# First attention of a two-layer decoder as a pipeline over single tiles, and the router's group ranks by halving

## Chip, cores and metric

The program runs on 1 core of one Trainium2 chip, in one launch. The metric is device time in microseconds (us) of that core, median of three runs for the kernel before.

## The reference, cut to what matters

The decoder has 8192 tokens (128 sequences of 64) of 128 features. It runs seven parts one after the other; two of them are touched here. The first attention replaces softmax by positive features of queries and keys (16 heads of 64):

```
q, k, v = x@Wq, x@Wk, x@Wv                      # 16 heads x 64
dash    = (data * 64**-0.25) @ proj.T
diag    = sum(data**2) * 64**-0.5 / 2
qf      = exp(dash - diag - max(dash, per head)) + 1e-6
kf      = exp(dash - diag - max(dash, over all)) + 1e-6
kv      = einsum('bnhm,bnhd->bhmd', kf, v)      # sums over the 64 tokens
num     = einsum('bnhm,bhmd->bnhd', qf, kv)
den     = einsum('bnhm,bhm->bnh', qf, sum(kf))
y1      = x + (num / den) @ Wo                  # then layer norm and feed forward
```

The last layer's router scores 64 experts for each token, in 8 groups of 8. A group's rank is the sum of its two best scores; the four best groups are kept, and the eight best experts in them.

```
group_scores = top_k(sfc.reshape(T, 8, 8), 2)[0].sum(-1)
_, gidx      = top_k(group_scores, 4)
```

## The kernel before

The tokens are 64 tiles of 128 (two sequences each). Every stage is a `Phase` with a program for each engine, written out by hand; engines meet at semaphores, and between two stages all engines meet at a barrier. So the order of the work on an engine is the order of the code.

`phase_performer` is the first attention. It handles two tiles (U = 2) per pass of its loop, 32 passes. Each projection of a tile (`wide`) is six matmuls of 512 columns: two halves of the 1024 features, three products each of high and low f16 parts. The five projections are q (Wq), k (Wk), v (Wv), and, through weights joined with `proj` beforehand, the features before the exponent (Wqp and Wkp). Each result fills two of the eight banks of PSUM. A pair of tiles has the buffers a0, b0, a1, b1, which are all eight banks, and every product of a tile goes through its own a or b: q and the query features first, then k over the query features, the transposed query features over q, and so on down to the output. The trace prints them as `b_a` and `b_b` without number. Since all banks belong to the pair in hand, TensorE starts q of a tile of the next pass only behind this line, when the tile's predecessor in the same buffers has been read for the last time:

```
pe.wait_ge(y_ready, before(it, j))
```

For each tile VectorE sums the squares of q (L567), takes the maximum per head (L569), joins both (L572), subtracts them from the query features (L574), sums the squares of k (L578), scales them (L580), subtracts them from the key features (L583), adds 1e-6 (L587), copies half of the sums over keys (L424), takes the reciprocals of den (L594, twice), multiplies (L597, twice) and adds x (L606). ScalarE squares q (L533), takes the exponent of the query features (L536), squares k (L540), copies the transposed query features (L543), takes the exponent of the key features (L546), copies v (L548), copies the other half of the sums (L551) and the transposed values (L555). TensorE's small products are: transposes of the query features (L479), sums over keys (L497), sums over features (L509), transposes of the values (L515), output (L520). The code runs each step for both tiles, then the next step for both.

The router's part is `rank_groups` in `phase_cross1`, the stage of the second layer's cross attention. A batch k is four tiles (N = 4), 16 batches in all; its steps on VectorE are spread over four columns of that stage's own pipeline, between the attention's steps. `after(k, step)` is a wait on VectorE's own semaphore plus an increment. The ranks of a batch take one MAX8 for every tile and group (32 of 8 elements each, eight sorted values out), then an addition of the first two.

## Time and profile before

| | us |
|---|---|
| runs of the kernel before | 4549.0 median, 4544.06 to 4552.46 (3 runs) |
| the profiled execution: its own time | 4554.91 |
| its span, first to last instruction | 4552.8 |
| first attention, 130 to 1158 us of the span | 1028.00 |
| TensorE busy in it | 835.96 |
| VectorE busy in it | 608.06 |
| ScalarE busy in it | 491.20 |
| stage with the router, 2880 to 3460 us | 580.00 |

The span lies 2.1 us below the time of its own execution, and that execution 5.9 us above the median. Busy time counts an instruction from its start to its modelled end; neighbours overlap, so the time from one start to the next says more of what an engine needs.

### The profile page before, as it was taken

What the parts mean: (1) busy time and instruction counts of PE and PEld (TensorE: products, weight loads), DVE (VectorE), ACT (ScalarE), POOL (GpSimd) and SP (SyncE); (2) the same over time, 40 slices, a digit from 0 to 9 for tenths busy, and PEclk for the clock granted to TensorE, in tenths of its full rate; (3) what the DMA queues carried; (4) which work ended last, traced back from release to release, by engine and by line L of the source; (5) the groups of instructions that cost most, each with busy time, mean ns of one, the idle gap of its engine ahead of it and who ended that gap; (6) DMA issues with size and microseconds to landing.
All of it is one profiled execution on the core that took longest, in us unless ns stands there. A gap on an engine that the chain in (4) does not pass through costs nothing. (4 is left out here: it accounts for less than half of the span.)

```text
span 4552.8 us, 96381 instructions
## 1 busy us (share of the span) xinstructions
PE 3746.1 (82%) x30771; PEld 2413.5 (53%) x30771; DVE 3298.2 (72%) x7642; ACT 2475.4 (54%) x6025; POOL 1914.2 (42%) x2753
## 2 busy tenths in 40 slices
PE   7788888888676777649898999788875999999998
PEld 3455555555444555436666666577762444444443
DVE  6655556565565666448888888588886888888888
ACT  1344444444664555337777777555544555555555
POOL 1000000000454666436556556111114778778777
PEclk9999999999886555556767777888877999999999
DMA  2000000000111111020000000122217566556664
GB/s 72 7 9 7 9 9 7 9 7 9 46 49 42 37 37 37 26 41 15 16 14 14 14 14 10 46 53 54 53 41 166 136 136 143 133 133 140 136 137 92
DMA packets 288788, 245.48 MB, mean 54 GB/s; under 512 B 60920, under 2 KB 216604, under 8 KB 288540
## 3 DMA queue, kind: packets, MB, share of 16 engines
q1 hardware_dynamic: 279452, 239.85, 22.2%
q10 hardware_dynamic: 9216, 4.20, 0.3%
q8 instruction: 55, 0.90, 0.1%
q14 instruction: 65, 0.53, 0.0%
HBM read 210.40 MB, written 33.55 MB: 54 GB/s over the span
## 5 line engine op out<-in xcount | busy, mean ns | idle before, releaser
L2536 POOL TENSOR_TENSOR d_hidden<-d_gated,d_upper 128x512 f32<-128x512 f32 x528 | 801.5, 1543 | 233.9 <-DVE d_upper L2645 110.3
L2652 DVE TENSOR_TENSOR d_h_low<-d_hidden,d_h_high 128x512 f16<-128x512 f32 x528 | 542.1, 1027 | 118.5 <-ACT d_h_high L2612 117.3
L2606 ACT ACTIVATE d_gated<-d_g 128x512 f32<-128x512 f32 x528 | 315.3, 597 | 466.1 <-PE d_u L2552 466.1
L684 POOL MEMSET f_minus_half<- 128x4 f32 x1 | 0.1, 102 | 1029.3 <-POOLq L37 1029.3
L2645 DVE TENSOR_TENSOR d_upper<-d_u,d_coef 128x512 f32<-128x512 f32 x512 | 349.4, 683 | 32.5 <-DMA d_coef<-coefT 13.0
L2612 ACT ACTIVATE d_h_high<-d_hidden 128x512 f16<-128x512 f32 x528 | 328.4, 622 | 8.2 <-POOL d_hidden L2536 8.2
L1719 ACT ACTIVATE c_sc<-c_sc,c_negmax 128x129 f32<-128x129 f32 x1024 | 326.1, 393 | 12.1 <-issue 9.5
L1547 POOL TENSOR_TENSOR c_posg<-w_pos,c_gate 128x512 f32<-128x512 f32 x256 | 265.7, 1038 | 0.0
L2550 PE MATMUL d_g<-d_x_high,w_Wg_high 128*128 128x512 f16 x528 | 200.9, 381 | 75.4 <-DVE d_upper L2645 38.4
L1626 PE MATMUL c_turned<-all_ident,c_sc 128*128 128x128 f32 x1024 | 232.4, 368 | 5.3 <-ACT c_sc L1719 4.8
L1724 ACT ACTIVATE c_pT<-c_turned 128x512 f32<-128x512 f32 x256 | 149.6, 584 | 154.7 <-PE c_turned L1626 154.7
L2550 PE MATMUL d_o<-d_h_high,w_Wd_high 128*128 128x512 f16 x528 | 200.1, 379 | 1.6 <-ACT d_h_high L2612 1.6
L2551 PE MATMUL d_u<-d_x_high,w_Wu_low 128*128 128x512 f16 x528 | 200.9, 380 | 0.0
L2550 PE MATMUL d_u<-d_x_high,w_Wu_high 128*128 128x512 f16 x528 | 200.8, 380 | 0.0
L2552 PE MATMUL d_g<-d_x_low,w_Wg_high 128*128 128x512 f16 x528 | 200.8, 380 | 0.0
L2551 PE MATMUL d_g<-d_x_high,w_Wg_low 128*128 128x512 f16 x528 | 200.8, 380 | 0.0
L2552 PE MATMUL d_u<-d_x_low,w_Wu_high 128*128 128x512 f16 x528 | 200.7, 380 | 0.0
L2552 PE MATMUL d_o<-d_h_low,w_Wd_high 128*128 128x512 f16 x528 | 200.1, 379 | 0.0
L2551 PE MATMUL d_o<-d_h_high,w_Wd_low 128*128 128x512 f16 x528 | 200.1, 379 | 0.0
L2048 POOL TENSOR_SCALAR d_rstd<-d_mv 128x1 f32<-128x1 f32 x64 | 13.9, 217 | 434.6 <-DVE d_mv L2269 434.6
L533 ACT ACTIVATE b_sq<-b_a 128x1024 f32<-128x1024 f32 x64 | 65.5, 1023 | 229.8 <-PE b_a L160 229.8
L1626 PEld LDWEIGHTS c_turned<-all_ident,c_sc 128*128 128x128 f32 x1024 | 150.8, 184 | 62.0 <-issue 50.2
(396 smaller groups left out, 10918.7 us busy)
## 6 DMA issues: line engine op xcount, KB each, us to landing
d_coef<-coefT SPq DMA_DIRECT2D x256, 512.0 KB, 7.7
d_cT<-in_ctxT SPq DMA_DIRECT2D x128, 64.0 KB, 2.0
mx_x<-in_xT SPq DMA_DIRECT2D x16, 256.0 KB, 2.8
b_x<-in_x SPq DMA_DIRECT2D x64, 64.0 KB, 1.8
y<-b_y SPq DMA_DIRECT2D x64, 64.0 KB, 1.6
f_y<-y SPq DMA_DIRECT2D x16, 256.0 KB, 3.3
f_x<-in_x SPq DMA_DIRECT2D x16, 256.0 KB, 3.9
x<-f_res SPq DMA_DIRECT2D x16, 256.0 KB, 2.4
```

The lines of the kernel that those rows point to most:

```text
L1547: nc.gpsimd.tensor_tensor(posg[a][:], w["pos"][:, hs, :], gate[s][:, hs].unsqueeze(2).to_broadcast([T, 4, T]), ALU.mult).then_inc(posg_rea ...
L1626: last = nc.tensor.transpose(tbank[a % 2][:, i, :], sc[slot(j)][:, 4 * a + i, 0:T], w["ident"][:])
L1719: last = nc.scalar.activation(sc[s][:, h, :], sc[s][:, h, :], ACT.Exp, bias=negmax[s][:, h:h + 1], scale=SCALE)
L1724: nc.scalar.activation(pT[slot(j)][:, 4 * a:4 * a + 4, :], tbank[a % 2][:], ACT.Copy).then_inc(pT_copied, 1)
L2536: nc.gpsimd.tensor_tensor(hidden[b][:], gated[b][:], upper[b][:], ALU.mult).then_inc(h_ready, 1)
L2550: nc.tensor.matmul(out, weights[0], high, start=start, stop=False)
L2551: nc.tensor.matmul(out, weights[1], high, start=False, stop=False)
L2552: return nc.tensor.matmul(out, weights[0], low, start=False, stop=stop)
L2606: nc.scalar.activation(gated[b][:], ps_g[i][:], ACT.Silu, scale=1.0 / W_SCALE).then_inc(silu_ready, 1)
L2612: nc.scalar.activation(h_high[b][:], hidden[b][:], ACT.Copy).then_inc(h_high_ready, 1)
L2645: nc.vector.tensor_tensor(upper[b][:], ps_u[i][:], coef[c % CBUFS][:, u % CU, :], ALU.mult).then_inc(upper_ready, 1)
L2652: nc.vector.tensor_tensor(h_low[b][:], hidden[b][:], h_high[b][:], ALU.subtract).then_inc(h_low_ready, 1)
```

## The change

`phase_performer` becomes a pipeline over single tiles. Column c of the pipeline does the projections and features of tile c, the sums over keys and over features of tile c-1 (`behind1`) and the normalising, transposing, output and addition of x of tile c-2 (`behind2`). The banks are dealt by role: `ps_a` takes q, then v, then k, then the transposed query features; `ps_b` takes the query features, then the key features; `ps_c` and `ps_d` take both kinds of sums, and `ps_d` the transposed values and the output. In SBUF every tensor keeps two slots. The products, their shapes and their number stay the same; TensorE, ScalarE, VectorE and the DMA queue get a new order, and the waits follow from it. There are 66 columns: four written out, a loop of 29 passes over two columns, four written out. Stores of y run two columns behind the loads of x, in the queue order store, load.

In the router, the 32 MAX8 and the addition of a batch become eleven operations over all groups at once: halves of a group are compared (4 with 4, 2 with 2, 1 with 1) and `high` and `low` carry the best and second best found so far. `after` has five steps where it had two before the ranks are added, and all later steps are renumbered.

```diff
--- before.py
+++ after.py
-        ps_a = [ph.ps(f"a{j}", [P, 2, 512]) for j in range(U)]
-        ps_b = [ph.ps(f"b{j}", [P, 2, 512]) for j in range(U)]
...
+        ps_a, ps_b, ps_c, ps_d = (ph.ps(n, [P, 2, 512]) for n in ("a", "b", "c", "d"))
...
+        def pipelined(eng, step):
+            def column(it, j):
+                step(*(None if isinstance(it, int) and not 0 <= U * it + j - back < TILES else (it, j - back) for back in range(3)))
+            for j in range(2 * U):
+                column(0, j)
+            with eng.Fori(2, steps - 1) as it:
+                for j in range(U):
+                    column(it, j)
+            for j in range(U + 2):
+                column(steps - 1, j)
...
+                def store(it, j):
+                    s, tile = slot(j), tile_of(it, j)
+                    sp.wait_ge(y_ready, nth(it, j))
+                    sp.sem_inc(waited, 1)
+                    sp.dma_start(y1[tile, :], y[s][:]).then_inc(stored[s], 16)
+                def load(it, j):
+                    sp.dma_start(x_sb[slot(j)][:], x[tile_of(it, j), :]).then_inc(loaded[slot(j)], 16)
+                def step(column, behind1, behind2):
+                    run(store, behind2)
+                    run(load, column)
+                pipelined(nc.sync, step)
...
+                def project_q(it, j):
+                    if not is_early(it, j, 1):
+                        pe.wait_ge(qfT_copied, nth(it, j) - 1)
+                    wide(it, j, ps_a, Wq).then_inc(q_ready, 1)
+                def features_q(it, j):
+                    if not is_early(it, j, 1):
+                        pe.wait_ge(dk_shifted, nth(it, j) - 1)
+                    wide(it, j, ps_b, Wqp).then_inc(dq_ready, 1)
+                def project_k(it, j):
+                    pe.wait_ge(v_copied, nth(it, j))
+                    wide(it, j, ps_a, Wk).then_inc(k_ready, 1)
+                def features_k(it, j):
+                    pe.wait_ge(dq_shifted, nth(it, j))
+                    wide(it, j, ps_b, Wkp).then_inc(dk_ready, 1)
+                def project_v(it, j):
+                    pe.wait_ge(q_squared, nth(it, j))
+                    wide(it, j, ps_a, Wv).then_inc(v_ready, 1)
+                def turn_features(it, j):
+                    pe.wait_ge(k_squared, nth(it, j))
+                    pe.wait_ge(q_exp, nth(it, j))
...
+                    last.then_inc(qfT_ready, 1)
+                def sum_keys(it, j):
+                    s = slot(j)
+                    pe.wait_ge(kf_ready, nth(it, j))
+                    if not is_early(it, j, 1):
+                        pe.wait_ge(y_ready, nth(it, j) - 1)
+                    pe.sem_inc(waited, 1)
...
+                    last.then_inc(kv_ready, 1)
+                def sum_features(it, j):
+                    s = slot(j)
+                    pe.wait_ge(kv0_copied, nth(it, j))
+                    pe.wait_ge(kv1_copied, nth(it, j))
+                    pe.sem_inc(waited, 1)
...
+                    last.then_inc(num_ready, 1)
+                def turn_values(it, j):
+                    pe.wait_ge(attn_done, nth(it, j))
...
+                    last.then_inc(turned, 1)
+                def output(it, j):
+                    pe.wait_ge(attn_ready, nth(it, j))
...
+                    last.then_inc(proj_ready, 1)
+                def step(column, behind1, behind2):
+                    run(features_q, column)
+                    run(project_q, column)
+                    run(turn_values, behind2)
+                    run(project_v, column)
+                    run(output, behind2)
+                    run(project_k, column)
+                    run(sum_keys, behind1)
+                    run(features_k, column)
+                    run(turn_features, column)
+                    run(sum_features, behind1)
+                pipelined(nc.tensor, step)
...
+                def step(column, behind1, behind2):
+                    run(square_q, column)
+                    run(copy_values, behind2)
+                    run(copy_v, column)
+                    run(exp_q, column)
+                    run(square_k, column)
+                    run(copy_sums, behind1)
+                    run(copy_features, column)
+                    run(exp_k, column)
+                pipelined(nc.scalar, step)
...
+                def norm_k(it, j):
+                    s = slot(j)
+                    dve.wait_ge(k_squared, nth(it, j))
+                    nc.vector.tensor_reduce(kn[s][:], sq[s][:], AX, ALU.add).then_inc(kn_ready, 1)
+                    dve.wait_ge(kn_ready, nth(it, j))
...
+                def shift_q(it, j):
+                    s = slot(j)
+                    dve.wait_ge(qn_ready, nth(it, j))
+                    dve.wait_ge(topped, nth(it, j))
+                    dve.sem_inc(waited, 1)
+                    nc.vector.scalar_tensor_tensor(q_shift[s][:], qn[s][:], DIAG, top[s][:], ALU.mult, ALU.add).then_inc(q_shift_ready, 1)
+                    dve.wait_ge(q_shift_ready, nth(it, j))
+                    nc.vector.tensor_tensor(e_sb[s][:], heads(ps_b), q_shift[s][:].unsqueeze(2).to_broadcast([P, H, DH]), ALU.subtract).then_inc(dq_shifted, 1)
...
+                def step(column, behind1, behind2):
+                    run(normalise, behind2)
+                    run(max_q, column)
+                    run(add_eps, behind1)
+                    run(norm_q, column)
+                    run(shift_q, column)
+                    run(add_x, behind2)
+                    run(copy_sums, behind1)
+                    run(norm_k, column)
+                    run(shift_k, column)
+                pipelined(nc.vector, step)
...
-                ROUTER_STEPS = 14
+                ROUTER_STEPS = 18
...
                 def rank_groups(k):
                     after(k, 1)
-                    for n in range(N):
-                        for g in range(G):
-                            last = nc.vector.max(best2[:, n, g, :], biased[:, n, 8 * g:8 * g + 8])
-                    last.then_inc(router_own, 1)
-                    after(k, 2)
-                    nc.vector.tensor_tensor(groups[:, :, 0:G], best2[:, :, :, 0], best2[:, :, :, 1], ALU.add).then_inc(router_own, 1)
-                    after(k, 3)
+                    eights = biased[:].rearrange("p n (g e) -> p n g e", g=G)
+                    nc.vector.tensor_tensor(high[0][:], eights[:, :, :, 0:4], eights[:, :, :, 4:8], ALU.max)
+                    nc.vector.tensor_tensor(low[0][:], eights[:, :, :, 0:4], eights[:, :, :, 4:8], ALU.min).then_inc(router_own, 1)
+                    for i in range(1, 3):
+                        a, b = slice(0, 4 >> i), slice(4 >> i, 8 >> i)
+                        after(k, 2 * i)
+                        nc.vector.tensor_tensor(mid[i][:], high[i - 1][:, :, :, a], high[i - 1][:, :, :, b], ALU.min)
+                        nc.vector.tensor_tensor(low[i][:], low[i - 1][:, :, :, a], low[i - 1][:, :, :, b], ALU.max).then_inc(router_own, 1)
+                        nc.vector.tensor_tensor(high[i][:], high[i - 1][:, :, :, a], high[i - 1][:, :, :, b], ALU.max)
+                        after(k, 2 * i + 1)
+                        nc.vector.tensor_tensor(low[i][:], low[i][:], mid[i][:], ALU.max).then_inc(router_own, 1)
+                    after(k, 6)
+                    nc.vector.tensor_tensor(groups[:, :, 0:G], high[2][:, :, :, 0], low[2][:, :, :, 0], ALU.add).then_inc(router_own, 1)
+                    after(k, 7)
...
```

TensorE in the loop of `phase_performer`, before, at the seam of two passes: transposes of the values of both tiles into a, output of both into b, and then q of the next pass into a. Of every `wide` the rows are L158, L159, L160, twice.

```order
L515 MATMUL b_a<-all_ident,b_attn 128x128 x16
L520 MATMUL b_b<-w_Wo,b_attnT 128x128 x16
L58 UNCONDITIONAL_BRANCH
L58 ISA
L158 ISA
L158 MATMUL b_a<-w_Wq_high,parts_xT_high 128x512
L159 MATMUL b_a<-w_Wq_low,parts_xT_high 128x512
L160 REGISTER_ALU
L160 MATMUL b_a<-w_Wq_high,parts_xT_low 128x512
```

TensorE in the loop after, around the output of tile c-2: it stands between v and k of tile c.

```order
L158 MATMUL b_a<-w_Wv_high,parts_xT_high 128x512
L159 MATMUL b_a<-w_Wv_low,parts_xT_high 128x512
L160 MATMUL b_a<-w_Wv_high,parts_xT_low 128x512
L537 MATMUL b_d<-w_Wo,b_attnT 128x128 x8
L158 MATMUL b_a<-w_Wk_high,parts_xT_high 128x512
L159 MATMUL b_a<-w_Wk_low,parts_xT_high 128x512
L160 MATMUL b_a<-w_Wk_high,parts_xT_low 128x512
```

Moved are the output (L520, now L537), out of a run of both tiles' small products into the middle of another tile's projections, and k and v, which now share the buffer a with q.

VectorE in the loop before: the k half of both tiles, from the sums of squares of k to the copies of sums (REGISTER_ALU rows make the value a wait compares with).

```order
L578 TENSOR_REDUCE b_stat<-b_sq 128x16
L85 REGISTER_ALU
L580 TENSOR_SCALAR b_stat<-b_stat,w_key_max 128x16
L85 REGISTER_ALU
L583 TENSOR_TENSOR b_kf<-b_a,b_stat 128x1024
L578 TENSOR_REDUCE b_stat<-b_sq 128x16
L85 REGISTER_ALU
L580 TENSOR_SCALAR b_stat<-b_stat,w_key_max 128x16
L85 REGISTER_ALU
L583 TENSOR_TENSOR b_kf<-b_a,b_stat 128x1024
L587 TENSOR_SCALAR b_kf<-b_kf 128x1024 x2
L424 COPY b_kv<-b_a 128x520 x2
```

VectorE in the loop after: the whole of a column but the reciprocals and products of tile c-2, which stand ahead of these rows; L609 and L643 belong to tile c-1, L663 to tile c-2.

```order
L624 TENSOR_REDUCE b_top<-b_b 128x16
L609 TENSOR_SCALAR b_kf<-b_kf 128x1024
L613 TENSOR_REDUCE b_qn<-b_sq 128x16
L631 SCALAR_TENSOR_TENSOR b_q_shift<-b_qn,b_top 128x16
L633 TENSOR_TENSOR b_e<-b_b,b_q_shift 128x1024
L660 REGISTER_ALU
L662 ISA
L663 TENSOR_TENSOR b_y<-b_d,b_x 128x128
L643 COPY b_kv<-b_c 128x520
L618 TENSOR_REDUCE b_kn<-b_sq 128x16
L620 TENSOR_SCALAR b_k_shift<-b_kn,w_key_max 128x16
L639 TENSOR_TENSOR b_kf<-b_b,b_k_shift 128x1024
```

Moved are the additions of 1e-6 (L587, now L609) and of x (L606, now L663) in between the query steps of tile c, and the copy of sums (L424, now L643) ahead of the sums of squares of k.

VectorE in `phase_cross1` before, at the ranks of a batch:

```order
L2252 TENSOR_TENSOR d_attn<-d_back,d_den 128x128
L2288 MAX d_best<-d_biased 128x8 x32
L2291 TENSOR_TENSOR d_groups<-d_best 128x4x8
L2294 MAX d_gtop<-d_groups 128x8 x4
L2257 TENSOR_TENSOR d_kB<-d_kT,w_variant 128x512
```

and after, in the same place:

```order
L2356 TENSOR_TENSOR d_high<-d_biased 128x128
L2357 TENSOR_TENSOR d_low<-d_biased 128x128
L2361 TENSOR_TENSOR d_mid<-d_high 128x64
L2362 TENSOR_TENSOR d_low<-d_low 128x64
L2363 TENSOR_TENSOR d_high<-d_high 128x64
L2365 TENSOR_TENSOR d_low<-d_low,d_mid 128x64
L2361 TENSOR_TENSOR d_mid<-d_high 128x32
L2362 TENSOR_TENSOR d_low<-d_low 128x32
L2363 TENSOR_TENSOR d_high<-d_high 128x32
L2365 TENSOR_TENSOR d_low<-d_low,d_mid 128x32
L2367 TENSOR_TENSOR d_groups<-d_high,d_low 128x4x8
L2370 MAX d_gtop<-d_groups 128x8 x4
```

The 32 MAX8 have given way to ten comparisons of 128, 64 and 32 elements, and the addition reads their results; what stands behind is the same.

## Rows read from the trace of the kernel before

**Rows 1.** The page's head and the granted clock, 40 equal slices of the span.

```profile
span 4552.8 us, 96381 instructions
...
PEclk9999999999886555556767777888877999999999
```

**Rows 2.** Busy time by stage; columns as its first line says, PEclk granted.

```profile
core 0: us, PE busy (x) PEld busy (x) DVE busy (x) ACT busy (x) POOL busy (x), PEclk, DMA share, GB/s
...
130.00:1158.00 1028.00, 835.96 (x12160) 555.46 (x12160) 608.06 (x896) 491.20 (x512) 0.82 (x2) 0.98 0.03 8
...
2880.00:3460.00 580.00, 434.24 (x4608) 380.65 (x4608) 450.12 (x1729) 307.49 (x923) 68.43 (x200) 0.78 0.22 60
```

**Rows 3.** Waits from 130 to 1158 us: total, times, longest.

```profile
ACT b_sq L533 <- PE b_a L160: 229.8, 64, 59.3
DVE b_y L606 <- PE b_b L520: 143.0, 64, 3.2
```

**Rows 4.** Timeline of VectorE, 480 to 545 us: start, length, instruction, idle before.

```profile
486.59 0.29 DVE L606 TENSOR_TENSOR b_y<-b_b,b_x 128x128 f32<-128x128 f32 x1 [3.16 <-PE b_b L520]
...
493.21 1.22 DVE L574 TENSOR_TENSOR b_e<-b_b,b_stat 128x1024 f32<-128x1024 f32 x1
...
500.20 1.22 DVE L578 TENSOR_REDUCE b_stat<-b_sq 128x16 f32<-128x1024 f32 x1 [2.04 <-ACT b_sq L540]
501.45 0.23 DVE L580 TENSOR_SCALAR b_stat<-b_stat,w_key_max 128x16 f32<-128x16 f32 x1
503.73 1.23 DVE L583 TENSOR_TENSOR b_kf<-b_a,b_stat 128x1024 f32<-128x1024 f32 x1 [2.04 <-PE b_a L160]
504.87 1.21 DVE L578 TENSOR_REDUCE b_stat<-b_sq 128x16 f32<-128x1024 f32 x1
...
510.94 0.70 DVE L424 COPY b_kv<-b_a 128x520 f32<-128x520 f32 x1 [0.66 <-PE b_b L497]
...
518.15 0.29 DVE L606 TENSOR_TENSOR b_y<-b_b,b_x 128x128 f32<-128x128 f32 x1 [3.16 <-PE b_b L520]
```

**Rows 5.** Timeline of ScalarE, 480 to 545 us.

```profile
489.56 1.02 ACT L533 ACTIVATE b_sq<-b_a 128x1024 f32<-128x1024 f32 x1 [3.92 <-PE b_a L160]
```

**Rows 6.** Timeline of TensorE, 482 to 512 us in pieces: first matmuls of runs.

```profile
483.49 0.98 PE L515 MATMUL b_a<-all_ident,b_attn 128*128 128x128 f32 x7 [0.42 <-DVE b_attn L597]
...
484.42 0.72 PE L520 MATMUL b_b<-w_Wo,b_attnT 128*128 128x128 f32 x5
...
487.99 0.38 PE L158 MATMUL b_a<-w_Wq_high,parts_xT_high 128*128 128x512 f16 x1
...
494.50 0.39 PE L158 MATMUL b_b<-w_Wk_high,parts_xT_high 128*128 128x512 f16 x1 [1.16 <-DVE b_e L574]
...
504.74 0.38 PE L158 MATMUL b_b<-w_Wv_high,parts_xT_high 128*128 128x512 f16 x1
...
506.03 0.38 PE L158 MATMUL b_b<-w_Wv_high,parts_xT_high 128*128 128x512 f16 x1
...
509.72 0.24 PE L497 MATMUL b_a<-b_v,b_kf 64*64 64x65 f32 x1 [0.20 <-ACT b_v L548]
...
510.67 0.22 PE L509 MATMUL b_a<-b_kv,b_qfT 64*64 64x65 f32 x1
```

**Rows 7.** Granted clock in stretches of 4 us, columns as in rows 2.

```profile
544.00:548.00 4.00, 3.00 (x56) 2.63 (x48) 2.51 (x6) 1.30 (x2) 0.00 (x0) 1.00 0.00 0
972.00:976.00 4.00, 1.74 (x8) 0.66 (x7) 2.96 (x4) 1.33 (x2) 0.00 (x0) 0.96 0.00 0
976.00:980.00 4.00, 3.98 (x20) 3.02 (x17) 1.45 (x2) 3.01 (x4) 0.00 (x0) 0.62 0.00 0
```

**Rows 8.** Timeline of VectorE around one ranking of groups in the router.

```profile
3013.61 2.27 DVE L2288 MAX8 d_best<-d_biased 128x8 f32<-128x8 f32 x32
3016.03 0.22 DVE L2291 TENSOR_TENSOR d_groups<-d_best 128x32 f32<-128x32 f32 x1
...
3024.16 0.29 DVE L2264 TENSOR_TENSOR d_y<-d_back,d_x_again 128x128 f32<-128x128 f32 x1
```

305 lines of the change are left out of this document (118 added, 187 removed).

## Prediction

> **What bounds the kernel now.** I read first the page's head, for the span and the clock [rows 1], then the busy times by stage [rows 2], since the change touches two stages alone. The first attention takes 1028 us, 23% of the span. No engine fills it: TensorE is busy 836 us, VectorE 608, ScalarE 491. So engines wait for each other, and the waits say how [rows 3]: ScalarE stands 230 us before it may square q, and VectorE 143 us before the last addition, both for TensorE. The timelines show the same place once per pass. The additions of x that end two passes lie 31.56 us apart (486.59 and 518.15 in [rows 4]), 15.78 us a tile. After the output TensorE starts q of the next pass at 487.99 [rows 6] and ScalarE can do nothing before 489.56 [rows 5]: when a pass ends and the next begins, one engine works and two stand.
>
> What TensorE needs for a tile follows from starts, not from busy time [rows 6]. A projection of six matmuls: 504.74 to 506.03, 1.29 us, five of them 6.45. Eight transposes: 483.49 to 484.42, 0.93, twice 1.86. Output of two tiles: 484.42 to 487.99, 1.785 each. Sums over keys: 509.72 to 510.67, 0.95; sums over features are as many matmuls of the same shape, 0.95. Together 12.0 us of 15.78. That is the floor: no product goes away. VectorE's instructions come to 608/64 = 9.5 us a tile, ScalarE's to 7.7 [rows 2]; neither can become the bound by its work.
>
> 32 passes of 31.56 us are 1010, so 18 of the 1028 us are something else: the start at a low clock, the edges, and falls of the clock. I counted twelve stretches of 4 us or pairs of them with a granted clock well below 1.00; one is 976 to 980 at 0.62, behind a stretch in which TensorE was busy 1.74 of 4 us [rows 7].
>
> **The change, part by part.** The new period is the longest closed chain through the three orders. I start a column with the query features at 0 on TensorE and take each time from a row.
> - q starts at 1.29, ScalarE squares it 1.57 later (487.99 to 489.56, [rows 5, 6]), at 2.86, for 1.02, to 3.88.
> - A handover to TensorE costs 0.07 (493.21 + 1.22 = 494.43 on VectorE, 494.50 on TensorE, [rows 4, 6]). v waits for the squares, as both use `ps_a`: 3.95. The transposes of tile c-2 (0.93) lie in that gap, from 2.58 to 3.51, so TensorE idles 0.44.
> - Then without a wait: output at 5.24, k at 7.02, sums over keys at 8.31.
> - VectorE copies them 1.22 after their start (509.72 to 510.94): 9.53. The sums of squares of k follow 0.09 before the copy's end, as 504.87 lies before 503.73 + 1.23 [rows 4]: 9.53 + 0.70 - 0.09 = 10.14. k was squared by 7.02 + 1.57 + 1.02 = 9.61, in time.
> - Scaling them starts 1.25 later (500.20 to 501.45), 11.39; the subtraction 0.23 + 0.03 later, 11.65; it lasts 1.23, to 12.88.
> - The next column's query features need `ps_b` back: 12.88 + 0.07 = 12.95.
>
> **So 12.95 us a tile**, 0.95 over the floor, in two idle pieces of 0.44 and about 0.5. The added waits hold the following. Query features of c wait for the key features of c-1 (this chain). Sums over keys wait for the addition of x of c-2, with the key features queued behind: output ends near 7.1, the addition 0.29 later, and the sums are due only at 8.31. Output waits for ScalarE's copy of the values: 2.58 + 1.1 + 1.02 = 4.7, and it is due at 5.24. q waits for the copy of the transposed features; these start at 10.55, so that is done near 12.7, before 14.24. In SP's queue each load stands behind a store that waits for y; it is wanted two columns later, 26 us. These are hidden; the thinnest cover is 0.5 us, and a copy 0.6 late would add 0.1 a tile, 6 us in all.
>
> 64 x 12.95 = 829. The last tile's rest beyond its column: in the old pass 8.7 us lie between its sums over keys and the end of an addition (509.72 to 518.44), with the exponent and 1e-6 ahead; I take 12, between 5 (TensorE's part alone) and 31 (a whole old pass). Of the 18 us of other time I keep 6: the start and the edges stay, but the falls followed idle stretches that the new column does not have; in 4 us of it TensorE stands at most 0.9. Stage: 829 + 12 + 6 = **847, 181 less**.
>
> **The router.** 32 MAX8 take 2.27 us, 0.07 apart, and with the gap of a wait the addition starts at 2.42 (3013.61 to 3016.03, [rows 8]). A `tensor_tensor` of 128 elements lasts about 0.29 and one of 32 about 0.22 [rows 8]; 64, not shown, lies between, 0.25. Independent ones overlap by 0.08, and `after` costs 0.15 of gap (3015.88 to 3016.03). Two of 128: 0.50; gap 0.15; the three of 64 and the dependent one 0.78, the wait between them mostly under the third; gap 0.15; the same of 32, 0.70; gap 0.15. Sum 2.43 against 2.42. If no overlap happened and all five gaps showed, the addition would come at 3.2, 0.8 us later; if more overlapped, 0.1 earlier. In 16 batches: 0, between -2 and +13 us. I take 0: the overlaps are visible in this stage.
>
> The sum against the profiled execution: 4554.9 - 181 = 4373.9 us. The median of the runs is 5.9 lower, so **4368**.
>
> **The rivals.**
> - *Longer handovers.* The chain has four places where one engine waits for another and two where VectorE waits for itself. Some waits are double now (sums over keys, subtraction). If each of the seven steps cost 0.13 more, the period is 13.85, 58 us more, 4426. If a further chain closes behind the loop, such as the copy of values late, 15 us is thinkable: 4499. For it speaks that a column mixes engines that the old pass kept in long runs; against it that the handovers of [rows 4 to 6] already stand beside other engines' work.
> - *The floor.* If the two idle pieces vanish, 64 x 12.0 = 768, stage 786, 4307. The chain above forbids it unless steps are shorter than their rows.
> - *The clock falls: slower.* TensorE becomes the bound, so its clock decides: the period is 12.0/c. At c = 0.76 it is 15.8 and the gain is gone; below that the kernel is slower than before. The slices of other stages go down to 0.5 to 0.7 [rows 1], and the router's stage has 0.78 with TensorE busy 434 of 580 us [rows 2]. If small pauses made it swing half of the time between 1.2 and 2.4 GHz, c = 0.75: 16.0 a tile, stage 1042, 4563; at 0.6 it is 4817. Against it: 544 to 548 us has TensorE busy 3.00 of 4 us, with small f32 products, at 1.00, and the falls came behind longer idleness [rows 7].
> - *It doesn't overlap.* If columns ran one tile after another as now, nothing changes: 4549. The waits of the code don't ask for that.
>
> The Trainium skill, page "TensorE: Matmul & The Clock Gate", section "A second HAM failure mode: psum-queue depth-cycling", speaks for the third: a kernel that cycles through PSUM banks leaves TensorE short idle times between groups of matmuls, and its clock then swings between the two levels. The new column has two such idle times. By the page the result would be the 4563 of that rival. The trace disagrees so far: handovers through the same banks in the old pass left the clock at 1.00 in the row named.
>
> **How the numbers follow.** Forecast 4335 to 4410: 0.74. Longer handovers, 4410 to 4520: 0.16. Clock, slower: 0.05. No overlap: 0.02. Below 4335, towards the floor: 0.03. A range of 4335 to 4435 holds the first and about half of the second, 0.82. 0.2%, 9 us, is about what a measurement of this kernel tells from no change. Faster: 0.74 + 0.16 + 0.03 = 0.93; same 0.02; slower 0.05.
>
> **What would show it.** In the changed trace, additions of x 12.95 us apart, one per tile; v starting 0.07 behind the squares of q, with 0.4 us idle ahead; query features starting behind the subtraction of the key features; granted clock 1.00 all through the stage; stage near 847 us; the ranks' addition 2.4 us after their first comparison. I would be wrong if TensorE's longest wait stood elsewhere (output, sums over keys), or if matmuls of 512 columns started 0.43 instead of 0.215 us apart for more than the stage's start.

## The result, and the profile after

The changed kernel takes 4405.1 us (median of 4 runs, 4399.8 to 4407.7) against 4550.7 us for the kernel before on the same chip: ratio 0.9675, 95% interval 0.9663 to 0.9687. The forecast was 4368, its range 4335 to 4435: inside the range and 37 us above the number. Of these 37 us, 26 are in the profiled executions, and they are the matter of what follows. The other 11 come from the step between profile and median: the profiled execution of the kernel before lay 5.9 us above its median, that of the changed kernel (4399.8) lies 5.3 below.

The page's head and the granted clock of the changed kernel, as in [rows 1]:

```profile
span 4397.7 us, 96050 instructions
...
PEclk9999999997865555577777777988869999999999
```

Busy time of the changed kernel in stretches, columns as in [rows 2]. The first row is the whole stage of the first attention:

```profile
130.00:996.00 866.00, 816.49 (x12160) 546.10 (x12160) 610.28 (x896) 500.93 (x512) 1.91 (x3) 0.99 0.04 10
...
200.00:300.00 100.00, 95.89 (x1398) 64.18 (x1400) 71.76 (x105) 59.05 (x61) 0.00 (x0) 1.00 0.03 10
...
700.00:800.00 100.00, 95.66 (x1374) 64.04 (x1375) 72.80 (x109) 59.46 (x62) 0.00 (x0) 1.00 0.03 9
```

The stage fell from 1028 us to 866, with the same instructions on every engine, and TensorE is busy 94% of it. The clock is 1.00 in each of the six stretches of 100 us from 200 to 800, of which two stand here.

The additions of x, which tell the period: the changed kernel's row in the list by tile, first over the whole stage and then from 560 to 700 us (shortest/median/longest ns, first and last start).

```profile
L663 DVE TENSOR_TENSOR b_y<-b_d,b_x x64: 290/292/293, 166.6 to 995.7; 128x128 f32<-128x128 f32 x64
...
L663 DVE TENSOR_TENSOR b_y<-b_d,b_x x11: 290/292/292, 562.5 to 694.4; 128x128 f32<-128x128 f32 x11
```

One addition per tile: (995.7 - 166.6)/63 = 13.16 us over the stage, (694.4 - 562.5)/10 = 13.19 in the middle of it. In [rows 4] a tile took 15.78; the forecast was 12.95. These are means. Single additions lie 12.96 and 13.42 apart by turns (509.72, 522.68 and 536.10 below), since a pass of the loop holds two columns; the 12.96 alone is not the forecast come true.

The changed kernel's timeline of TensorE, the first matmul of each run in one column and of the next column, as in [rows 6]:

```profile
502.28 0.39 PE L158 MATMUL b_b<-w_Wqp_high,parts_xT_high 128*128 128x512 f16 x1 [0.27 <-DVE b_kf L639]
...
503.58 0.38 PE L158 MATMUL b_a<-w_Wq_high,parts_xT_high 128*128 128x512 f16 x1
...
506.24 0.39 PE L158 MATMUL b_a<-w_Wv_high,parts_xT_high 128*128 128x512 f16 x1 [0.32 <-ACT b_sq L561]
...
507.54 1.95 PE L537 MATMUL b_d<-w_Wo,b_attnT 128*128 128x128 f32 x16
509.33 0.38 PE L158 MATMUL b_a<-w_Wk_high,parts_xT_high 128*128 128x512 f16 x1
...
510.72 0.27 PE L514 MATMUL b_c<-b_v,b_kf 64*64 64x65 f32 x1
...
515.51 0.39 PE L158 MATMUL b_b<-w_Wqp_high,parts_xT_high 128*128 128x512 f16 x1 [0.27 <-DVE b_kf L639]
```

ScalarE squaring q in this column and in the next:

```profile
505.16 1.03 ACT L561 ACTIVATE b_sq<-b_a 128x1024 f32<-128x1024 f32 x1 [1.92 <-PE b_a L160]
...
518.31 1.03 ACT L561 ACTIVATE b_sq<-b_a 128x1024 f32<-128x1024 f32 x1 [1.85 <-PE b_a L160]
```

VectorE in the same column, from the addition of x through the subtraction that frees `ps_b`, and the two additions behind it:

```profile
509.72 0.29 DVE L663 TENSOR_TENSOR b_y<-b_d,b_x 128x128 f32<-128x128 f32 x1 [0.66 <-PE b_d L537]
511.95 0.70 DVE L643 COPY b_kv<-b_c 128x520 f32<-128x520 f32 x1 [1.94 <-PE b_d L514]
512.56 1.21 DVE L618 TENSOR_REDUCE b_kn<-b_sq 128x16 f32<-128x1024 f32 x1
513.81 0.23 DVE L620 TENSOR_SCALAR b_k_shift<-b_kn,w_key_max 128x16 f32<-128x16 f32 x1
514.15 1.23 DVE L639 TENSOR_TENSOR b_kf<-b_b,b_k_shift 128x1024 f32<-128x1024 f32 x1
...
522.68 0.29 DVE L663 TENSOR_TENSOR b_y<-b_d,b_x 128x128 f32<-128x128 f32 x1 [0.47 <-PE b_d L537]
...
536.10 0.29 DVE L663 TENSOR_TENSOR b_y<-b_d,b_x 128x128 f32<-128x128 f32 x1 [0.66 <-PE b_d L537]
```

Read these together from 502.28: it is the forecast's chain, link by link. q 1.30 later; ScalarE squares it from 505.16 to 506.19 and v starts at 506.24, 3.96 (forecast 3.95); output at 5.26 (5.24); k 7.05 (7.02). Then the links grow. Sums over keys at 8.44 (8.31), so 1.39 us behind k where a projection takes 1.29. The copy 1.23 and the reduction 0.61 behind are as forecast. The subtraction comes 0.34 behind the scaling, forecast 0.26. It ends at 515.38, and the query features start 0.13 later, forecast 0.07. Three links give 0.10 + 0.08 + 0.06 = 0.24 us a column. The column shown is 13.23 us long (502.28 to 515.51), with 0.04 more in small steps; the next is 13.15, as ScalarE starts 1.49 behind q there (516.82 to 518.31) and not 1.58 (forecast 1.57). The two alternate, and their mean is the 13.19.

Waits of the changed kernel from 130 to 996 us, which answer to [rows 3]:

```profile
ACT b_sq L561 <- PE b_a L160: 181.1, 64, 62.9
DVE b_kv L643 <- PE b_d L514: 130.0, 64, 2.4
...
DVE b_y L663 <- PE b_d L537: 46.2, 64, 6.1
...
PEld b_a L158 <- ACT b_sq L561: 35.6, 64, 2.1
...
PE b_b L158 <- DVE b_kf L639: 17.9, 63, 1.8
```

TensorE's two named waits (PEld is its weight loads) are those of the forecast: for the squares of q ahead of v, and for the subtraction ahead of the query features.

The router, the changed kernel's VectorE around one ranking, as in [rows 8]:

```profile
2853.24 0.29 DVE L2356 TENSOR_TENSOR d_high<-d_biased 128x128 f32<-128x128 f32 x1
...
2853.88 0.23 DVE L2361 TENSOR_TENSOR d_mid<-d_high 128x64 f32<-128x64 f32 x1
2854.02 0.22 DVE L2362 TENSOR_TENSOR d_low<-d_low 128x64 f32<-128x64 f32 x1
...
2855.54 0.19 DVE L2367 TENSOR_TENSOR d_groups<-d_high,d_low 128x32 f32<-128x32 f32 x1
```

The addition starts 2.30 us behind the first comparison, in all 16 batches between 2.28 and 2.31; before it was 2.42 (2.40 to 2.42).

**What the forecast had no term for** stands in the last stage, the experts, whose code the change does not touch. First the weight load of `d_g`, by tile, of the kernel before and of the changed one, then of the changed kernel ScalarE's waits from 3330 to 4330 us and the instruction queue in the whole stage (3276 to 4398 us):

```profile
L2550 PEld LDWEIGHTS d_g<-d_x_high,w_Wg_high x528: 95/98/151, 3461.1 to 4535.7; 128*128 128x128 f16 x176
```

```profile
L2626 PEld LDWEIGHTS d_g<-d_x_high,w_Wg_high x528: 95/98/152, 3296.3 to 4380.6; 128*128 128x128 f16 x176
```

```profile
ACT d_gated L2682 <- PE d_u L2628: 406.8, 467, 2.3
ACT d_gated L2682 <- issue: 22.6, 5, 6.4
```

```profile
q14 instruction: 44, 0.36, 0.1%
```

From the first to the last load 1084.3 us, before 1074.6: 10 us more for the same work. ScalarE stood five times, 4.5 us each on average, with nothing to wait for that the profile shows, some 137 us apart. The loop's branch is met six times, from 3562.1 to 4248.3 us; the stands follow the five that lead back to its start and not the last. Queue 14, which carries instructions in packets of 8 KB, moved 44 of them, against 18 in the kernel before (3440 to 4553 us; 20 with the two at the program's end), which has no such stand of ScalarE. Between 3660 and 4360 us, in the middle of the loop, the kernel before has 3 of its packets, the changed one 5 or 6 in every 140 us.

### The profile page after: what moved, and what is told of

Same layout as the page of the kernel before. It is cut to its first block and busy times, and to the rows that moved or that the text cites. A ratio compares the mean times of both kernels' runs of the same rounds, so it can differ in the third digit from the quotient of the medians.

```text
span 4397.7 us, 96050 instructions
## 1 busy us (share of the span) xinstructions
PE 3699.9 (84%) x30771; PEld 2374.2 (54%) x30771; DVE 3292.1 (75%) x7290; ACT 2486.9 (57%) x6025; POOL 1921.4 (44%) x2753
## 5 line engine op out<-in xcount | busy, mean ns | idle before, releaser
L1692 PE MATMUL c_turned<-all_ident,c_sc 128*128 128x128 f32 x1024 | 214.9, 346 | 16.8 <-ACT c_sc L1785 14.8
L1897 DVE TENSOR_REDUCE c_top<-c_sc 128x4 f32<-128x516 f32 x256 | 176.9, 691 | 8.8
L1692 PEld LDWEIGHTS c_turned<-all_ident,c_sc 128*128 128x128 f32 x1024 | 139.8, 173 | 76.9 <-issue 41.9
```

The source lines that it names most:

```text
L1692: last = nc.tensor.transpose(tbank[a % 2][:, i, :], sc[slot(j)][:, 4 * a + i, 0:T], w["ident"][:])
L1897: m = own.mark(nc.vector.tensor_reduce(top[s][:, hs], sc[s][:, hs, :], AX, ALU.max))
```

## The experiments

All ran beside the kernel before, and a ratio is to its runs on the same chip, whose medians were 4549.0 to 4553.2 us. A single run has no interval. "Last stage" is from the first to the last weight load of `d_g`; the expectations count from the end of the stage before to the end of the program, 37 us more. "Packets" are those of queue 14 from the first such load to the end. The period is that of the additions of x in the middle of the stage.

| kernel | median us (runs) | ratio to before, 95% | period | last stage | packets |
|---|---|---|---|---|---|
| before | 4550.7 (4) | | 15.78 | 1074.6 | 20 |
| changed | 4405.1 (4) | 0.9663 to 0.9687 | 13.19 | 1084.3 | 44 |
| attn_only | 4407.1 (5) | 0.9672 to 0.9697 | | 1092.8 | 44 |
| router_only | 4571.4 (6) | 1.0032 to 1.0056 | | 1101.6 | 44 |
| router_pad86 | 4553.6 (11) | 0.9994 to 1.0014 | | 1071.6 | 20 |
| pad88 | 4383.2 (5) | 0.9621 to 0.9646 | | 1075.9 | 19 |
| q_first | 4372.1 (5) | 0.9599 to 0.9624 | 12.76 | 1090.0 | 44 |
| q_first_pad88 | 4355.6 (5) | 0.9555 to 0.9581 | | 1073.0 | 19 |
| norm_k_twice | 4482.9 (1) | | 14.38 | 1089.0 | 44 |
| norm_q_twice | 4410.1 (1) | | 13.26 | 1092.0 | 44 |
| wait_moved | 4398.2 (1) | | 13.20 | 1084.7 | 44 |
| turn_first | 4374.3 (5) | 0.9595 to 0.9621 | 12.95 | 1073.3 | 19 |
| pad24 | 4407.3 (1) | | | 1092.5 | 44 |
| pad256 | 4413.4 (1) | | | 1090.2 | 44 |

### One part at a time

attn_only is the new first attention with the old ranks; router_only the old attention with the new ranks. The edit is the change's own pieces, for attn_only:

```diff
-                    nc.vector.tensor_tensor(high[0][:], eights[:, :, :, 0:4], eights[:, :, :, 4:8], ALU.max)
...
+                    for n in range(N):
+                        for g in range(G):
+                            last = nc.vector.max(best2[:, n, g, :], biased[:, n, 8 * g:8 * g + 8])
```

> The new attention with the router's old ranks. Theory: the gain is the attention's alone; columns 13.2 us apart as in the full change, the stage 161 us shorter than before, and the last stage (experts), whose code nobody touched, some 10 us longer than before, since ScalarE's program is the same 40 instructions longer as in the full change. Total about 145 us below before. Rival (the ranks carry part of it): the stage with the router was 7 us shorter after the change, so without the new ranks this kernel would lie 7 us above the full change. By the ranks' own timeline (0.15 us a batch) only 2 us.

> The old attention with the new ranks. By the ranks' own timeline, 0.15 us for each of 16 batches: 2 us less than before, within noise. By the stage's length in the two traces: 7 us less. Last stage as before, since ScalarE's program has the length of before: no reloads of instructions in its loop.

The attention alone gives 4407.1, the whole change 4405.1: it is the gain. Its last stage is 18 us longer than before in the profiled execution, where some 10 were expected. The ranks alone, expected 2 to 7 us faster, make the kernel slower, 4571.4, by 0.3 to 0.6%, although the addition comes 2.30 us behind the first comparison there too. Their loss is not in the router's stage but in the last one, 1101.6 against 1074.6 us. VectorE's waits there in router_only, then in the run below that mends it (3480 to 4500 us):

```profile
DVE d_upper L2655 <- issue: 27.4, 5, 5.7
DVE d_upper L2655 <- PE d_u L2562: 10.5, 20, 1.5
```

```profile
DVE d_upper L2657 <- PE d_u L2564: 5.4, 15, 0.5
```

Here it is VectorE that stands five times. Its program has 86 instructions fewer than before, ScalarE's is unchanged.

### Where the last stage's loop stands

The theory: what the change alters for the last stage is only where its code lies. ScalarE's loop of 341 instructions starts at its instruction 1833 in the kernel before and at 1873 in the changed one; VectorE's, 312 long, starts at 2804 before, 2781 in the changed kernel and 2718 in router_only. The padding is increments of a semaphore that nobody waits for:

```diff
                 pipelined(nc.scalar, step)
+                for _ in range(88):
+                    act.sem_inc(waited, 1)
```

In router_pad86 the same stands at the end of VectorE's first attention, with 86 and `dve.sem_inc`; in pad24 and pad256 the number is 24 and 256.

> The full change with 88 increments of a semaphore on ScalarE behind its last step of the attention; nothing else. Everything behind stands 88 instructions later in ScalarE's program, 128 later than before in all. Theory: the last stage got longer because ScalarE's loop there (341 instructions) now straddles one more piece of its instruction memory and is loaded again in every pass (43 packets on queue 14 in that stage against 17); shifted to a multiple of 128 it should not be: about 17 packets, stage 10 us shorter, total 8 us below the full change (88 increments cost 2 to 4 us at the seam). Rival (chance, or the memory traffic of that execution): no change of the packets, and the time equal or 3 us longer.

> The kernel before with the new ranks of the router alone, and 86 semaphore increments at the end of VectorE's first-attention program, so that VectorE's loop of the last stage stands at the same instruction (2804) as in the kernel before; nothing of the work is left out. Theory of placement (the new ranks make VectorE's program 86 instructions shorter, the loop of the last stage then starts at 2718 and its instructions are fetched again in every pass): the five waits for an instruction stream ahead of the upper part in that stage, 27 us together, go away, the last stage takes 1112 us instead of 1139, about 20 instruction packets on queue 14 in it instead of 44, and the median falls from 4571 to 4546 to 4552, ratio to before near 1.000. Rival (the last stage is longer by the new ranks' data or by chance of the execution): it stays at 4571, ratio 1.0044. The 86 increments themselves cost at most 86 times 0.06 us, 5 us, once.

> The whole change with 24 semaphore increments at the end of ScalarE's first-attention program, so that its loop of the last stage starts at instruction 1897; nothing of the work is left out. One look: the last stage and its packets on queue 14 count. Starts at 1833 and 1961 gave about 1112 us and 20 packets, a start at 1873 gave 1121 to 1130 us and 44. If the loop of 341 instructions is fetched again in every pass when it lies over three blocks of 256 instructions and not when it lies over two, then 1833, 1873 and 1961 put the border so that 1897 is bad as well: 44 packets, five instruction waits on ScalarE, last stage 1121 to 1130. If any pause or any padding cures it, 20 packets and 1112.

> The whole change with 256 semaphore increments in the same place, so that the loop starts at 2129, which is 1873 plus 256; nothing of the work is left out. One look, the last stage counts (the increments themselves may cost up to 20 us once, at the end of the first attention). If blocks of 256 instructions decide, the place is as bad as that of the whole change: 44 packets and 1121 to 1130 us, although 88 increments gave 19 packets and 1113. If a longer distance from the start of the program is what helps, or any padding, 20 packets and 1112.

88 increments take 22 us off the changed kernel (19 if each is compared through its own kernel before), where 8 were expected, and the packets above those of before go too. 86 on VectorE bring router_only back to the time of before: 4553.6 against 4553.2 on that chip, just over the 4546 to 4552 expected. 24 leave ScalarE's loop at 1897 with 44 packets and five stands of 3.7 to 5.9 us (the profile puts one down to TensorE), and 256, which put it at 2129 = 1873 + 256, are as bad as none. So neither a pause nor the amount of padding cures it: the place does. ScalarE's waits in the last stage of pad24, then of pad256:

```profile
ACT d_gated L2684 <- issue: 20.2, 4, 5.9
```

```profile
ACT d_gated L2684 <- issue: 23.8, 5, 5.7
```

Starts at 1833 and 1961 are good, 1873, 1897 and 2129 bad. The Trainium skill, page "Runtime: NRT & Kernel Launch", section "Instruction fetch mechanics", says that most engines hold two blocks of 256 instructions and that a branch to a block outside them has to fetch it first. By that rule a loop of 341 fits when it lies over two blocks and not when it touches a third, and all five starts fit one position of the borders (bad when the start plus 91 to 130, modulo 256, is over 171); the trace agrees, in the eight profiled kernels with a bad start of ScalarE's loop alone as in router_only. What the profiles show without the rule: a bad place of ScalarE's loop makes the last stage 8 to 21 us longer in one execution, and costs 22 us by the medians of the changed kernel and pad88.

The paddings have a price of their own, read from the stages behind: from the last addition of x to the first `b_bn` two stages on, the feed-forward stage between, it takes 12 us more in pad256 and 8 more in router_pad86, and in pad88 nothing. The traces record the increments themselves: on ScalarE they start 0.07 us apart (256 from 988.97 to 1006.78 us), on VectorE 0.10 (86 from 1156.29 to 1164.60). ScalarE is done with its tiles before VectorE and TensorE, and the 6 us that the 88 of pad88 take cost nothing.

### Is the chain closed?

Two kernels give VectorE the same extra work, 1.21 us a column, at two places. norm_k_twice:

```diff
+                    nc.vector.tensor_reduce(spare[s][:], sq[s][:], AX, ALU.add)
                     nc.vector.tensor_reduce(kn[s][:], sq[s][:], AX, ALU.add).then_inc(kn_ready, 1)
```

norm_q_twice has the same ahead of the reduction into `qn`.

> The whole change, with the sums of squares of k taken twice per column (the first into a tile that nobody reads); the result is the same. One look: the period of the columns in the first attention counts. If the closed chain is right, in which these sums stand between the copy of the sums over keys and the scaling with nothing to hide them, the period grows from 13.2 us by the whole of the second reduction: by its 1.25 us of time from start to start, less nothing, to 14.4, and the stage from 866 to about 943. Rival (TensorE's own work is the bound and the chain has slack): the period grows by less than 0.4.

> The whole change, with the sums of squares of q taken twice per column (the first into a tile that nobody reads); the result is the same. One look. VectorE gets as much more work as when the sums of k are taken twice, but ahead of the shift of the query features, where TensorE's key features wait next at 9.3 us of the column. By the chain the period stays at 13.2 to 13.4 us if the shift of the query features and the addition of x have that much slack. If VectorE's total work were the bound the period would grow by about 1.2, as with k.

Additions of x by tile, 560 to 700 us, first of norm_k_twice, then of norm_q_twice:

```profile
L665 DVE TENSOR_TENSOR b_y<-b_d,b_x x9: 290/292/293, 573.6 to 688.6; 128x128 f32<-128x128 f32 x9
```

```profile
L665 DVE TENSOR_TENSOR b_y<-b_d,b_x x11: 280/281/283, 565.4 to 698.0; 128x128 f32<-128x128 f32 x11
```

(688.6 - 573.6)/8 = 14.38 against (698.0 - 565.4)/10 = 13.26: on k the period grows by 1.19, on q by 0.07, out of the same work. Between its first and its second sums norm_k_twice shows what each column pays:

```profile
576.44 1.21 DVE L619 TENSOR_REDUCE b_spare<-b_sq 128x16 f32<-128x1024 f32 x1
577.57 1.21 DVE L620 TENSOR_REDUCE b_kn<-b_sq 128x16 f32<-128x1024 f32 x1
```

The start-to-start of 1.13 is nearly all of the 1.19. The chain over the sums of k is closed with no slack, and VectorE's total work is not the bound.

### Breaking the chain

q_first lets TensorE issue q ahead of the query features, so that the subtraction has 1.29 us more before anything waits for it:

```diff
                 def step(column, behind1, behind2):
-                    run(features_q, column)
                     run(project_q, column)
+                    run(features_q, column)
```

> The full change with TensorE's column begun by q and then the query features. Theory (closed chain): what holds the column is the chain from the query features over q, v, output, k, sums over keys, the copy, sums of squares of k and the subtraction back to the query features; q does not need the buffer that this chain frees, so q first takes 1.3 us out of the way and the column falls from 13.2 to about 12.75 us, 27 us in all, held then by TensorE's own work and the wait for the squares of q. Rival (TensorE is full already, the idle time is only how its starts are drawn): 13.2 us and no gain.

> The whole change, with q issued before the query features on TensorE, and with 88 semaphore increments at the end of ScalarE's first-attention program; nothing of the work is left out. If the two gains found apart (33 us by the order in the column, 22 by ScalarE's placement) have separate causes they add up: 4405 - 33 - 22 = 4350, last stage 1113 us, attention stage 834. If the gain of the padding came from something else in the run, it does not add: 4372.

The additions of x of q_first, 560 to 700 us, and TensorE's waits from 200 to 800, of its weight loads and of its matmuls:

```profile
L663 DVE TENSOR_TENSOR b_y<-b_d,b_x x11: 278/278/280, 570.9 to 698.5; 128x128 f32<-128x128 f32 x11
```

```profile
PEld b_d L537 <- ACT b_attnT L590: 14.7, 47, 0.3
...
PE b_a L158 <- ACT b_qfT L578: 9.4, 47, 0.2
```

The period is 12.76, and the wait for the subtraction is gone. Two others show now: output's for the copy of the values, which the forecast had covered by 0.5 us, 0.31 a time, and q's for the copy of the transposed query features, 0.20 a time. Which of the two would have to go first was not tried. The stage takes 834 us (130 to 964), 32 less, where 27 were expected: 0.43 x 64 is 27.5, the rest lies at its edges. With the padding the two gains add up nearly: 4355.6 against the 4350 expected, ratio 0.9568, the fastest version here.

### The small links

wait_moved tries to take back the 0.08 ahead of the subtraction, which has two waits:

```diff
                     dve.wait_ge(kn_ready, nth(it, j))
...
+                    dve.wait_ge(dk_ready, nth(it, j))
...
                 def shift_k(it, j):
-                    dve.wait_ge(dk_ready, nth(it, j))
                     dve.wait_ge(k_shift_ready, nth(it, j))
```

(The added line stands ahead of the wait for `kn_ready` in `norm_k`.)

> The whole change, with VectorE's wait for the key features moved up from ahead of the subtraction to ahead of the scaling of the sums of squares, where it stands behind a 1.21 us reduction; nothing of the work is left out. One look, the period of the columns counts. If the subtraction starts 0.34 us behind the scaling, and not 0.26 as in the kernel before, because two waits stand ahead of it, the gap goes back to 0.26 and, as the chain has no slack, the period falls from 13.2 by the same 0.08 to 13.1, the stage by 5 us. Rival (the 0.34 is the size of the operands or the pool's semaphore, not the second wait): 0.34 and 13.2 stay.

VectorE in wait_moved:

```profile
576.94 1.21 DVE L618 TENSOR_REDUCE b_kn<-b_sq 128x16 f32<-128x1024 f32 x1
578.26 0.23 DVE L621 TENSOR_SCALAR b_k_shift<-b_kn,w_key_max 128x16 f32<-128x16 f32 x1
578.52 1.23 DVE L639 TENSOR_TENSOR b_kf<-b_b,b_k_shift 128x1024 f32<-128x1024 f32 x1
```

The subtraction now follows the scaling by 0.26, as hoped, but the scaling follows the reduction by 1.32 instead of 1.25, and the period stays at 13.20. The half of the expectation on the gap held, the half on the period failed: a reduction of 1.21 us ahead does not hide the wait.

Nor is the number of waits the cause. The kernel before waits twice ahead of its subtraction too, for the key features and for its own scaling. Where both were there in time the subtraction came 0.27 behind the scaling:

```profile
506.12 0.23 DVE L580 TENSOR_SCALAR b_stat<-b_stat,w_key_max 128x16 f32<-128x16 f32 x1
506.39 1.23 DVE L583 TENSOR_TENSOR b_kf<-b_a,b_stat 128x1024 f32<-128x1024 f32 x1
```

Of two waits one stands in an instruction of its own, which the timeline leaves out and the trace records. In the kernel before it is the wait for TensorE's key features, passed at 506.13 while the scaling ran. In the changed kernel it is the wait for VectorE's own scaling: it starts at 514.08, 0.27 behind the scaling, and the subtraction follows 0.07 later. In wait_moved a wait of this kind, for VectorE's own reduction, stands ahead of the scaling (578.19, the scaling at 578.26). So the 0.07 belongs to a wait for the engine's own last result that stands by itself, and moving the other wait within the chain moved it along. A version with that wait on the subtraction itself was not run.

turn_first adds to q_first_pad88 the moved wait, and turns the query features ahead of the key features:

```diff
                     run(sum_keys, behind1)
-                    run(features_k, column)
                     run(turn_features, column)
+                    run(features_k, column)
```

> q ahead of the query features, ScalarE's 88 semaphore increments and the moved wait as in the runs of their names, and on TensorE the turning of the query features ahead of the key features, so that these cover less and the transposes fall into the time in which VectorE works at the sums of k; nothing of the work is left out. With q first the period is 12.76 us. By starts read from its trace the closed chain then runs over ScalarE's squares, VectorE's shift of the query features and their exponent; with the transposes moved up I expect 12.65 us, 7 us off the stage, and the moved wait hidden: 4348, between 4340 and 4356. If the transposes wait for the exponent of the query features (0.3 us late or more), the period grows and the run is slower than 4356.

The expectation of 4340 to 4356 failed. It took 4374.3 us, 19 more than q_first_pad88 on another chip (ratio 0.9608 against 0.9568), period (699.1 - 569.6)/10 = 12.95; 64 times the difference in the period is 12 us. TensorE in turn_first:

```profile
571.78 1.09 PE L502 MATMUL b_a<-all_ident,b_e 128*128 128x128 f32 x8 [0.24 <-ACT b_sq L566]
572.71 0.38 PE L158 MATMUL b_b<-w_Wkp_high,parts_xT_high 128*128 128x512 f16 x1
```

The transposes do wait, not for the exponent as the expectation's second case had it but for the squares of k, with which they share `ps_a`, and the key features queue behind them. The exponent has its part all the same: ScalarE starts these squares at 570.72, at the end of the exponent (569.76, 1.06 long), without a wait between. VectorE then waits 0.78 for these ahead of the scaling: the moved wait has made it stand earlier too. How much of the loss is due to either edit wasn't tried apart.

## Why the prediction was right, and where it was short

**The mechanism held step by step.** Column by column, one addition per tile; v starts 0.05 behind the squares of q, query features behind the subtraction, the chain's order as forecast, and norm_k_twice against norm_q_twice shows that this chain and not VectorE's work sets the period. The 4374 us of profiled time that the sum gave compare with 4399.8 of the profiled execution, 26 more: 19 in the first attention, 10 in the last stage, 8 less in the router's, and 5 more spread over the stretches between. That the last stage and the router's nearly cancel is luck: the forecast had 0 for either.

**The period, 12.95 forecast, 13.19 measured: 0.24 x 64 = 15 us.** The step that was short is the pricing of three links by rows of the old pass: the small sums of 64 rows started 1.39 us behind the first matmul of k, not 1.29; the subtraction 0.34 behind the scaling, not 0.23 + 0.03; the query features 0.13 behind its end, not 0.07. The prediction took each of these steps from a place where what lengthens it here was absent. The second is the wait for VectorE's own scaling that stands by itself, as the records of the changed kernel and of wait_moved show (above). The third looks alike: the wait for the subtraction stands in a register instruction of its own (515.41, 0.05 long) and the first weight load at 515.51 behind it, while ahead of v, as at 494.50 in the kernel before, the weight load itself waits. For the first the wait was over 0.67 us earlier (the sums over keys wait for the addition of x, done at 510.01); what comes late is the weight load of 64 rows, 0.52 behind the last one of k:

```profile
510.19 0.10 PEld L160 LDWEIGHTS b_a<-w_Wk_high,parts_xT_low 128*128 x1
510.71 0.13 PEld L514 LDWEIGHTS b_c<-b_v,b_kf 64*64 64x64 f32 x1 [0.42 <-issue]
```

A load of 128 rows follows the last one of the key features by 0.22 in the same column (512.69 to 512.90). No run puts the first or the third to the test. The prediction had named a direction ("some waits are double now") and put it in a rival at 0.13 for each of seven steps. It was three steps at 0.06 to 0.10, and the reason given was wrong: both steps named there, sums over keys and subtraction, wait twice in the kernel before as well.

**Edges and falls of the clock, 12 + 6 us forecast:** 865.7 - 64 x 13.19 = 21.5 for both. Stage 847 against 866: 15 from the period, 4 from here.

**The clock rival did not come.** 1.00 in all of 200 to 800 us, where TensorE is busy 96 of each 100 us and stands twice a column, 0.32 and 0.27 in the rows above. By the Trainium skill, page "TensorE: Matmul & The Clock Gate", section "A second HAM failure mode: psum-queue depth-cycling", weighed in the prediction, the 4563 us of that rival would have come; the trace disagrees, since the new column cycles through the same banks with short idle pieces at a granted clock of 1.00. The floor of 4307 did not come either, and its 12.0 us a tile was too low: it has 0.95 for each kind of small sums, where the sums over keys alone add 1.39 - 1.29 + 1.09 = 1.19. Adding the shortest steps of the changed kernel, q_first and turn_first gives 12.4 (an estimate for a column without any wait), and q_first, with two waits left, came to 12.76.

**The router, 0 forecast:** the addition comes 0.12 us sooner, 2 us in 16 batches, as the sum of 2.43 for the new ranks was 0.13 too high. The stage shows somewhat more: from ScalarE's first to its last `d_res` 490.0 us against 497.5, and in the other profiles 487.2 to 493.0 with the new ranks and 494.5 in attn_only with the old. By medians they are worth 2 us beside the new attention (4405.1 against 4407.1, which is within what the runs scatter) and some 8, the price of the padding, in router_pad86. So 2 to 8 us, at or below the low end of the -2 to +13 given; what beyond the 2 at the addition makes them stays open.

**The last stage, no term in the forecast:** 10 us in the profiled execution, 22 by the medians of pad88 and the changed kernel. The prediction costed what the changed parts do and never what they do to code behind them. Both parts move the experts' loops: the attention moves ScalarE's to a bad place, the ranks alone move VectorE's to one, and together VectorE's is at a good one, which is why attn_only and the whole change are alike and router_only is slow. With the placement mended the change takes 4383.2 us, against 4368 forecast. The 15 us that remain are as many as the period's; the smaller terms (4 at the edges, 5 between the stages, 8 less in the router's) about cancel.

## What to carry to other kernels

When a change makes a program longer or shorter, look at the loops behind it: compare the instruction packets in their stretch and the waits put down to "issue", before a difference of some tenths of a per cent is read as the worth of the edit. An edit that gained a little in its own stage was +0.4% here for this reason alone, and 88 idle increments were worth 0.4 to 0.5%.

In a pipeline over engines, write the longest closed chain and count each wait in it at its price, those that stand in an instruction of their own above all; then test it by the same extra work once on the chain and once beside it. What to change next is the order at the place where the chain closes (q_first), not the load of the engines; and a wait that is moved along the chain is still in it.

## What the runs showed of the hardware that was not expected

- A loop whose code lies badly is fetched again in each pass: 44 packets of 8 KB instead of 18 to 20, and one stand of 4 to 6 us behind each branch back to its start, on ScalarE (22.6 us in five) or VectorE (27.4 in five). Moving a 341-instruction loop from 1833 to 1873 brought it, 1961 removed it, and 2129, 256 further than 1873, brought it back.
- A wait of VectorE for its own last result costs 0.07 us where it stands in an instruction by itself (0.34 instead of 0.27 from scaling to subtraction), even behind an instruction of 1.21 us (1.32 instead of 1.25). A second wait that is over before the instruction ahead ends costs nothing that shows (0.27 in the kernel before).
- Semaphore increments that stand alone start 0.07 us apart on ScalarE (256 in 17.8 us) and 0.10 on VectorE (86 in 8.3 us).
- The first of the f32 matmuls with 64 rows starts 0.10 us later behind an f16 projection than another projection would (1.39 against 1.29, with their weight load 0.52 behind the last one of the projection, where a load of 128 rows follows in 0.22), and they take 1.09 us until the next projection starts (510.72 to 511.81 in the changed kernel), where the old pass had 0.95 between the sums over keys and the sums over features [rows 6].
